# A decoder layer on one core: shared experts moved into the recurrence bodies, Gram products moved ahead, one tile pipeline over both parts, another order of the first loads

## The reference

```
q, k, v = silu(dwconv(hs @ W.T))                       # 4 heads of 64; beta = sigmoid(hs @ Wb.T)
# delta rule in chunks: A = tril(kb @ k.T, -1); Tinv = (I + A)^-1; u = Tinv @ v; w = Tinv @ kb
u_i = u_i - w_i @ S;  o_i = q_i @ S + attn @ u_i;  S = S + k_i.T @ u_i
wgt = softmax(gelu([hs, short.mean, long.mean, delta.mean] @ fg_w1.T + b1) @ fg_w2.T + b2)
x = x + rmsnorm(wgt0*short + wgt1*long + wgt2*delta + wgt3*v) @ Wo.T
x = x + cross_attention(layernorm(x), ctx)             # 16 heads of 16
# experts: sigmoid router, top 2 of 8, each y_e = (silu(x @ G_e.T) * (x @ U_e.T)) @ D_e.T, times the mean
# weight of expert e; two shared experts take every row
x = x + sum_e(sel_e * y_e * wmean_e) + shared(layernorm(x))
```

## Time and profile before

| what | value |
|---|---|
| median of the timed runs | 1503.44 us |
| profiled execution, whole / span | 1505.3 / 1503.2 us |
| PE matmul busy, span share | 1132.4 us, 75% |
| DVE busy | 867.0 us, 58% |
| POOL busy | 554.8 us, 37% |
| ACT busy | 454.0 us, 30% |
| mean granted clock of PE | 0.887 of 2.4 GHz |
| DMA | 124.56 MB, mean 83 GB/s |

### The profile page before, as it was taken

The page is one execution under the profiler, slowest core; times in us unless marked ns, Lnnn a source line. Parts: engine busy times, 40 slices in busy tenths (PEclk is TensorE's granted clock), DMA queues, the critical chain, the costliest instruction groups (busy, mean ns, idle before and its releaser), DMA issues. The chain is left out here.

```text
span 1503.2 us, 21723 instructions
## 1 busy us (share of the span) xinstructions
PE 1132.4 (75%) x7496; PEld 854.1 (57%) x7496; DVE 867.0 (58%) x2140; ACT 454.0 (30%) x818; POOL 554.8 (37%) x948
## 2 busy tenths in 40 slices
PE   1888878392993895797498399299389699788996
PEld 0455557371872773575476286287276567567553
DVE  1887844253755655566466476475567555543555
ACT  1766644222212322312312222221231244323110
POOL 2233434437018217415433542721822120303064
PEclk9998889696997897799699599699689899998999
DMA  6344342501002102000200210210200533446174
GB/s 160 91 142 136 118 123 89 173 1 56 15 2 102 43 1 99 33 10 31 87 29 29 70 43 15 88 43 1 70 29 29 211 118 97 159 136 211 50 232 142
DMA packets 85786, 124.56 MB, mean 83 GB/s; under 512 B 29040, under 2 KB 64112, under 8 KB 83504
## 3 DMA queue, kind: packets, MB, share of 16 engines
q1 hardware_dynamic: 78768, 104.30, 21.4%
q0 software_dynamic: 6912, 18.88, 3.9%
HBM read 66.91 MB, written 56.24 MB: 82 GB/s over the span
## 5 line engine op out<-in xcount | busy, mean ns | idle before, releaser
L900 ACT ACTIVATE arena<-bank 128x512 f32<-128x512 f32 (+2 forms) x318 | 166.3, 544 | 541.7 <-PE bank L541 132.2
L388 PE MATMUL bank<-const,arena 128*128 128x128 f32 x256 | 42.6, 321 | 212.4 <-DVE arena L1840 166.0
L388 PEld LDWEIGHTS bank<-const,arena 128*128 128x128 f32 x256 | 34.2, 164 | 219.1 <-DVE arena L1840 168.9
L1411 DVE SCALAR_TENSOR_TENSOR arena<-arena,param 128x512 f32<-128x512 f32 x144 | 106.1, 749 | 35.8 <-ACT arena L923 32.2
L405 PE MATMUL bank<-hsT,wt 128*128 128x512 f32 x192 | 100.5, 681 | 24.2 <-ACT hsT L900 24.2
L1283 POOL TENSOR_TENSOR arena<-arena 128x126 f32<-128x126 f32 (+22 forms) x248 | 101.0, 407 | 22.2 <-DVE arena L1482 3.3
L1270 POOL COPY arena<-arena 32x512 f32<-32x512 f32 x32 | 33.8, 1056 | 192.9 <-DVE arena L1472 191.4
L1335 POOL DMA_INDIRECT arena<-slots_y,arena x64 | 61.6, 962 | 114.2 <-DVE xt L1932 60.4
L1285 POOL TENSOR_TENSOR arena<-arena 128x126 f32<-128x126 f32 (+22 forms) x248 | 93.7, 378 | 19.4
L609 PEld LDWEIGHTS bank<-arena 128*128 128x128 f32 x768 | 88.6, 192 | 5.9 <-issue 5.7
L609 PE MATMUL bank<-arena 128*128 128x128 f32 x768 | 89.3, 275 | 0.0
(11 more groups left out here) (262 smaller groups left out, 2706.9 us busy)
## 6 DMA issues: line engine op xcount, KB each, us to landing
arena<-slots_x SPq DMA_DIRECT2D x78, 128.0 KB, 2.1
slots_y<-arena SPq DMA_DIRECT2D x78, 128.0 KB, 1.7
xt<-x_in SPq DMA_DIRECT2D x16, 512.0 KB, 5.5
kq_T<-kq SPq DMA_DIRECT2D x8, 1024.0 KB, 3.9
kq<-kq_T SPq DMA_DIRECT2D x8, 1024.0 KB, 7.3
vT<-v_T SPq DMA_DIRECT2D x8, 514.0 KB, 3.9
hs_T<-hsT SPq DMA_DIRECT2D x8, 512.0 KB, 4.2
v_T<-vT SPq DMA_DIRECT2D x8, 512.0 KB, 4.2
```

Of the source, the lines that this page charges most:

```text
L388: last = tr(o[:, t * P:(t + 1) * P], src[:, t, c * P:(c + 1) * P], ident)
L900: free(act.activation(out_, in_, func, **kw), name)
L1411: ins = V.scalar_tensor_tensor(cv[:, k % 4, :], pre[:, j, d:d + GT], param[:, at + d:at + d + 1], cv[:, k % 4, :], ALU.mult, ALU.add)
```

## The change

Four edits, one file.

*Shared experts.* `late_in` and `late_out` (PE), `late` and `late_added` (DVE), `late` (ACT) do the shared experts of group i-1 inside body i, behind the router, from the rows that are still in `xnT`; the sum is added to `xt` before it is stored (`rows_added`). The weights are loaded again in each body into a free half of `attnT` (`late_w`). The stores and loads of `xnT` in DRAM, `shared`, and `load_fx` go away.

*Gram products and recursion.* Steps t = 0 and 1 of the loop do two Gram products each. POOL copies the diagonal blocks tile by tile (16 copies in place of 4), clears them behind the `pow`s, and computes the router's norm factor within the recursion, behind step k = 15. The recursion of group 0 runs on DVE (`first_solve`).

*One tile pipeline.* Tiles 0 to 77 run without a break; DVE adds one 128-row piece of the final sum in 15 of the last steps (`PIECES`), the other 17 pieces follow.

*Start.* Rows of group 0 and the first 1536 columns of `wt` are loaded first; PE and ACT wait for less; POOL's first norm factor comes ahead of its 61 tap copies; DVE scales weights and masks behind the first convolution.

```diff
-    "gram_ready": 16, "diag_ready": 4, ...
+    "gram_ready": 16, "diag_ready": 16, ...
@@ PE
-            pe.wait_ge(w_loaded, 16 * 3)
-            pe.wait_ge(setup_dve, N_DVE_SETUP)
-            pe.wait_ge(setup_pool, N_POOL_SETUP)
             hidden_rows(0)
+            pe.wait_ge(first_loaded, 16)
...
+            def late_in(i, up_banks):
+                pe.wait_ge(sem("late_w_loaded"), 16 * min(i + 1, NG - 1))
+                for s_, at in (("lg", 0), ("lu", 1)):
+                    for e in range(2):
+                        n = f"{s_}{e}.{i}"
+                        w_ = expert(i, e)[at]
+                        k = up_banks[e] if at else None
+                        o = open_bank(pe, n, next(cross_bank) if k is None else k)
+                        for c in range(CK):
+                            last = mm(o[:, :], w_[:, c, :], xnT[:, c, :], start=c == 0, stop=c == CK - 1)
+                        full(last, n)
+            def late_out(i, banks_):
+                for e in range(2):
+                    drained(pe, f"lu{e}.{i}")
...
                 for t in range(T):
-                    if ahead:
-                        front_gram(i + 1, t)
+                    if ahead and t < 2:
+                        front_gram(i + 1, 2 * t)
...
                     if t < 2:
                         gate_hidden(0, 1 + t)
+                        if ahead:
+                            front_gram(i + 1, 2 * t + 1)
...
+                filters(2)
+                filters(3)
                 if x:
                     routing()
-                filters(2)
-                filters(3)
+                    late_in(i - 1, (7, None))
+                    late_out(i - 1, (2, 3))
                 pe.wait_ge(sem("on_ready"), i + 1)
@@ ACT, body
                 done(act.activation(gw[:, 1, :, :], gw[:, 0, :, :], ACT.Exp), "exp_ready")
+                if x:
+                    late()
+                    router()
...
-                if ahead:
-                    front_blocks(i + 1)
-                if x:
-                    router()
                 for c in range(CK):
                     n = f"oT{c}.{i}"
                     o = filled(act, n)
                     evac(h1T[:, c, :], o[:, :], n)
+                if ahead:
+                    front_blocks(i + 1)
@@ POOL
-                if x is not None:
-                    norm_scale(1, "x", 2 * x + 2)
+            def front_steps(i, x=None):
                 pool.wait_ge(sem("units_ready"), i + 1)
                 for k in range(QB - 1, 0, -1):
...
+                    if k == 15 and x is not None:
+                        norm_scale(1, "x", 2 * x + 2)
@@ DVE
                 dve.wait_ge(sem("gate_ready"), 2 * i + 2)
+                if x:
+                    routing()
                 for t0 in range(0, T, 2):
...
                 if x:
-                    routing()
+                    late()
...
                 done(ins, "on_ready")
                 if x:
+                    late_added()
                     ranks(i - 1)
...
             long_turned(0)
             front_units(0)
+            first_solve()
             long_turned(1)
...
+                if n in PIECES:
+                    combines(1)
```

More of the change, by code:

```diff
@@ L45 @@
 TILE0 = (0, NTILE[0], NTILE[0] + NTILE[1])
+PIECES = tuple(s for s in range(TILE0[1] + 5, TILE0[2] + 1) if s % 6)
 NWORD3 = (max(NTILE) + 2) // 3
@@ L872, in _ @@
             routing()
-            steps(4)
+            steps(2)
+            late_in(NG - 1, (None, None))
+            steps(2)
+            late_out(NG - 1, (None, None))
             positions(NG - 1)
-            steps(NTILE[0] + 3 - 31)
-            tile_experts(1)
-            for s_ in range(-2, NTILE[1] + 1):
-                tile_step(1, s_)
+            steps(8)
             n = "weights.0"
-            for i in range(NG):
-                shared(i)
-                if i == 0:
-                    o = open_bank(pe, n, next(cross_bank))
-                    pe.wait_ge(sem("route_sums"), 1)
-                    full(mm(o[:, 0:E], cst("ones"), gw[:, 0, :, :].rearrange("p t k -> p (t k)")[:, 0:E],
-                            start=True, stop=True), n)
+            o = open_bank(pe, n, next(cross_bank))
+            pe.wait_ge(sem("route_sums"), 1)
+            full(mm(o[:, 0:E], cst("ones"), gw[:, 0, :, :].rearrange("p t k -> p (t k)")[:, 0:E],
+                    start=True, stop=True), n)
+            steps(TILE0[2] + 1 - at_step[0])
         @block.scalar
@@ L1025, in router, with late @@
                          "scores_ready")
-                return rows, probs, routing, router
+                def late():
+                    for e in range(2):
+                        n = f"lg{e}.{i}"
+                        o = filled(act, n)
+                        evac(late_g[i][e], o[:, :], n, ACT.Silu)
+                return rows, probs, routing, router, late
             def body(i, x, ahead):
                 if x:
-                    rows, probs, routing, router = x
+                    rows, probs, routing, router, late = x
                 for t in range(T):
@@ L1132, in steps @@
                 for _ in range(k):
-                    tile_step(0, at_step[0])
+                    tile_step(at_step[0])
                     at_step[0] += 1
-            rows, probs, routing, router = cross(NG - 1)
+            rows, probs, routing, router, late = cross(NG - 1)
             steps(5)
@@ L1590, in routing, with late, late_added @@
                                          prm("lb").unsqueeze(1).broadcast_to([P, T, E]), ALU.add), n)
-                return masks, rows2, anykey, queries, context, scores, values, row_stats, rows3, routing
+                def late():
+                    for e in range(2):
+                        n = f"lu{e}.{i}"
+                        o = filled(dve, n)
+                        drained(dve, f"lg{e}.{i}")
+                        free(V.tensor_tensor(late_h[i][e], o[:, :], late_g[i][e], ALU.mult), n)
+                def late_added():
+                    for k in range(2):
+                        n = f"ld{k}.{i}"
+                        o = filled(dve, n)
+                        dst = rows[:, 2 * k:2 * k + 2, :]
+                        free(V.tensor_tensor(dst, dst, o[:, :].rearrange("p (t d) -> p t d", t=2), ALU.add), n)
+                    for k in range(2):
+                        drained(dve, f"ld{k}.{i}")
+                    done(V.memset(spare[:, :], 0.0), "rows_added")
+                return (masks, rows2, anykey, queries, context, scores, values, row_stats, rows3, routing, late,
+                        late_added)
             def ranks(i):
@@ L1693, in body @@
                 if x:
-                    masks, rows2, anykey, queries, context, scores, values, row_stats, rows3, routing = x
+                    (masks, rows2, anykey, queries, context, scores, values, row_stats, rows3, routing, late,
+                     late_added) = x
                     masks()
@@ L1867, in _ @@
                 body(i, cross(i - 1) if i else None, i + 1 < NG)
-            masks, rows2, anykey, queries, context, scores, values, row_stats, rows3, routing = cross(NG - 1)
+            (masks, rows2, anykey, queries, context, scores, values, row_stats, rows3, routing, late,
+             late_added) = cross(NG - 1)
             NT_ = NG * T
```

384 lines of the change are left out of this document (185 added, 199 removed).

## The result

The changed kernel takes 1465.5 us (median of four executions, 1463.6 to 1470.5) beside 1503.3 us for the kernel before on the same chip: ratio 0.9754, 95% interval 0.9727 to 0.9781. The forecast was 1468. The time came out close, but two of its terms were wrong by much and in opposite directions, so the profile has to be read term by term. The profiled execution took 1463.9 us.

A forecast was written before the change was run, and what follows sets the result against it. Four limits in turn: a late start, waiting chains in the bodies, PE in the tiles, PE then DVE at the end. Terms -16+0-3+39+0+11-66 = -35 us against 1503.2 gave 1468, range 1437 to 1491.

The forecast's parts named there:

- start, until the first Gram product: Start: early rows let PE begin at about 12.8 us, 19.6 earlier; after DVE's scaling and SP's store, -16 us.
- first recursion, until the first N: Group 0's recursion on DVE: 17.7 us against 28.6 on POOL, but transposes stand behind it, so 0 us gained.
- body 0: Body 0: no cross part, only the earlier recursion; -3 us (bounds 0 and -4).
- bodies 1 to 6: Bodies 1 to 6: recursion 4.4 us earlier, yet each body longer by 6.5 us; +39 (bounds +11 and +54).
- tiles, until the first gather: Tiles: group 7's shared experts (10.6 us, 1.6 hidden), weight sums and the filled pipeline delay the first gather, +11 us.
- end: First gather to end: POOL's gathers limit at 1.25 us each; 86.6 us instead of 152.5, -66.
- The factor: Bodies 1 to 6: router's norm factor behind k = 15 moves turned rows, gate and mix back by 13.5 us.
- Earlier recursion: Body 3: with memsets and factor out of its way, the recursion starts 4.4 us earlier, despite 0.9 for paired Gram products.
- The mix: Body 3: DVE's mix starts at 724.1 and its factors are done at 734.0 us in the trace, after router and filters.
- `late_out`: Body tail on PE: shared experts' second matmuls, behind `late` and ahead of the mixed rows, charged 5.9 us.
- The signs: Marks expected in the profile after: first N at 270 to 272, row norm waiting 12 to 14 us, bodies of 124 to 129.
- light-bodies rival: Bodies: shared matmuls keep PE at full clock and a body costs only 1.8 us or less; total 1440, chance 0.2.

The follow-up runs named there:

- Kernel 8: Changed kernel with the rows of groups 0 and 1 issued behind weights, masks and start rows again: 1509.6 us, beside 1498.5 for the changed kernel rerun.
- kernel 4: Changed kernel with the first group's recursion on GpSimd again instead of DVE: 1494.1 us, beside 1498.5 for the changed kernel rerun.
- kernel 1: Changed kernel with the router's norm factor behind step k = 28 of the recursion instead of k = 15: 1470.0 us, beside 1498.5 for the changed kernel rerun.
- kernel 3: Changed kernel with one Gram product in each of the four steps instead of pairs: 1484.1 us, beside 1498.5 for the changed kernel rerun.
- kernel 2: Changed kernel with the norm factor behind k = 28, `late` ahead of DVE's compaction and ACT's placing ahead of its copies: 1463.2 us, ratio to before 0.9548.
- 10: Changed kernel with early factor, `late` and placing first, single Gram products, first recursion on GpSimd and tile numbers read word by word: 1443.0 us, ratio to before 0.9419.
- kernel 11: As kernel 10, but the mixed rows' two pow inside GpSimd's recursion, compaction behind `late_added`, ACT's copies first again: 1436.5 us, ratio to before 0.9378.
- Kernel 6: Changed kernel without the shared experts of groups 0 to 6 in the bodies (not the whole layer): 1482.6 us, beside 1498.5 for the changed kernel rerun.
- kernel 7: Changed kernel with all 32 pieces of the final sums behind the last tile: 1517.7 us, beside 1498.5 for the changed kernel rerun.
- kernel 9: The changed kernel unedited, run again on a later chip: 1498.5 us, ratio to before 0.9789.

## Why the forecast came out, and where it was wrong

The sum was -35, the profiled execution shows -41.1. By the forecast's steps:

| step | forecast | measured |
|---|---|---|
| start, until the first Gram product | -16 | -15.0 |
| first recursion, until the first N | 0 | +2.7 |
| body 0 | -3 | -1.4 |
| bodies 1 to 6 | +39 | +14.7 |
| body 7, until the first tile | 0 | +1.5 |
| tiles, until the first gather | +11 | +19.5 |
| end | -66 | -63.2 |

- **Start: right.** PE at 12.57 (12.8 said). Kernel 8 shows that 12.4 of the 19.9 us are the early rows. That every engine waits for the last mask and the last weights, as my opening has it, is the smaller part: without the early rows the start gains only about 7 us.
- **First recursion: the mechanism right, the size off.** I worked out 17.7 us for DVE; it took 19.8, and the compaction came 3.4 us later than the 266.0 I had: 2.1 us by the length, the rest because the recursion began 15.2 us earlier than before (237.69 against 252.97) and not 17. That the transposes behind it eat the gain is what kernel 4 shows.
- **The factor: right.** I said 18 us behind the recursion's start and a wait of 12 to 14; it was 17.5 and 14.8, and the turned rows moved by 14.3 us behind N (13.5 said). Half clock there: as said, but it costs less. I charged 2.8 us for transposes and logits; they took 1.97 and 2.71 instead of 1.09 and 1.95, 1.6 together, for the full clock is back within the logits. The mix began at 102.5 behind N, I had 103.6. That the gate had slack of just that size was not right: kernel 1 takes the wait away and a body gets 5 us shorter.
- **Earlier recursion: right, 3.8 us instead of 4.4.** The forecast took the Gram pairs for +0.9 us; kernel 3 has them at 1.5 to 2.4. I then credited them with the 3.8 in kernel 3's expectation, though the page said otherwise.
- **The mix: mis-sized.** I carried over 9.9 us from its first product to the factors. It took 8.0 in the changed kernel. Neither before nor after does DVE stand idle within it; some of its own operations got shorter. Groups of DVE from 340 to 1200 us (busy, mean ns of one), two of the kernel before, two of the changed one, one of kernel 1:
```profile
L1819 DVE SCALAR_TENSOR_TENSOR arena<-arena,gw 128x256 f32<-128x256 f32 x32 | 18.7, 623 | 0.0
L1815 DVE SCALAR_TENSOR_TENSOR arena<-bank,gw,arena 128x256 f32<-128x256 f32 x32 | 13.8, 472 | 0.0
...
L1894 DVE SCALAR_TENSOR_TENSOR arena<-arena,gw 128x256 f32<-128x256 f32 x30 | 13.5, 491 | 0.0
L1890 DVE SCALAR_TENSOR_TENSOR arena<-bank,gw,arena 128x256 f32<-128x256 f32 x29 | 12.6, 474 | 0.0
...
L1894 DVE SCALAR_TENSOR_TENSOR arena<-arena,gw 128x256 f32<-128x256 f32 x30 | 18.0, 638 | 0.0
```
  The products with both inputs in the arena (SBUF) were slow in the kernel before, where the mix ran beside GpSimd's longest recursion steps (120 to 136 elements). With the factor late the mix lies beside the last, short steps and behind the recursion, and they are fast; those that read a PSUM bank don't change. Kernel 1 moves the mix back beside the long steps, and it takes 9.9 us again. Kernels 1, 2, 10 and 11, with the factor early, all have 9.7 to 9.9 in body 3; the changed kernel, 3 and 6 have 8.0. The filters, which the change moved ahead of the mix in all of them, make no such difference. Mix and factors were done at 110.4 behind N, I had 113.5.
- **`late_out`: mis-sized, and its return left out of the bound.** I charged 5.9 us; it took 5.1 in body 3 and 5.1 to 5.4 in all six bodies. (In the later runs some bodies have up to 6.8, on each of the three chips.) The full clock it hands on to mixed rows and projection I did count. Together, with compaction and `late` 0.3 us shorter than I had, the mixed rows start at 117.3 and not at 121.5: 1.1 us by the clock ahead of the mix and what follows it, 1.9 by the mix, 0.3, and 0.9 by late_out. These 4.2 us in body 3 are the error of a body, 4.0 on the mean. Kernel 6 confirms the account from the other side: taking all shared work out shortens a body by 1.4 us only.
- **The tiles: a step missing.** Nothing of the 10.6 us of group 7's matmuls was hidden (I let 1.6), and SyncE's reading of the tile numbers had been harmless when part 0 was drained before part 1; a pipeline that runs through made it a hole of 5.7 us. I had put 1.5 on that boundary. The first two tiles run at half clock (two transposes 0.66 us instead of 0.41), 1.3 us that I hadn't counted, and the 1 us that I took off for the stores doesn't show.
- **The end: right.** Gathers are the limit, without a gap, 1.27 us each instead of 1.25, and kernel 7 shows that they need the pieces where they are.
- **The signs.** First N at 274.8 (270 to 272 said) and a body of 122.9 us (124 to 129 said) both missed, the one late and the other short, and the row norm's wait, 14.8 us, lies just above its 12 to 14. The others came as said. Why body 0 gained 1.4 us and not 3, and body 7 lost 1.5, was not followed up.

So the total came close because bodies 1 to 6 were over-charged by 24 us and all other steps together under-charged by 18. That the two cancel is luck. The light-bodies rival (1.8 us a body) was nearest to what the bodies do, while its total of 1440 is not, for the same reason.

The Trainium skill (TensorE: Matmul & The Clock Gate, What's actually happening) puts the cost of the ramp under 1% of a typical kernel's span. The rows don't bear that out as a rule for a kernel with chains like this one, where the half clock comes back in each body: in kernel 2 the projection alone takes 6.35 us instead of 3.69 in body 3, in kernel 11 N takes 2.3 us more, and both come back in body 4 (6.0 us for the projection in kernel 2); six times 2.3 to 3.6 us is 1 to 1.5% of the span. The Trainium skill (GPSIMD Engine Reference, 4.1 Engine selection) has GpSimd about twice as slow for two-input elementwise work; here the first group's 62 operations take 19.8 us on VectorE and 28.6 on GpSimd (kernel 4, 239.77 to 268.34), a ratio of 1.4.

## What to carry to other kernels

Where a chain on one engine is made to carry a small step of another chain, put it where its input is just ready, not halfway: a factor of 1.3 us placed 13 us too late (92.6 us behind N, in kernel 1 79.4) moved an idle gap and cost 28 us in all. Before charging work that fills an idle gap at its full length, ask what clock the work behind it had without it. Before carrying over a length, ask what ran beside it on the other engines, and whether it still will. And when a drain between two phases is taken out, look for what the queues did in its shadow: register reads, waits for tables.

## What the runs showed of the hardware

- **Two places of the tiles, and 2% of the whole.** On the three later chips every kernel is slow at the same two places: from tile 28 to 36 it takes 28.2 to 29.1 us (17.4 in the first comparison), from tile 55 to 60 23.0 to 24.9 us (9.0). PE, ACT and DVE have waits there that nothing in the profile explains, while GpSimd's gathers go on every 1.25 us at the second. PE in kernel 9:
```profile
1402.65 0.48 PE L850 MATMUL bank<-const,arena 128*128 128x128 f32 x1 [3.23 <-issue]
1406.39 1.22 PE L855 MATMUL bank<-arena 128*128 x2 [3.27 <-issue]
1409.76 0.69 PE L835 MATMUL bank<-const,arena 128*128 128x128 f32 x2 [2.15 <-issue]
```
  These two places make 27 of the 33 us between the first comparison and kernel 9. What they are was not tried, and whether it is the chip at all stays open; the kernel before is 28 us slower there, with no trace of it to say where.
- **VectorE is slower beside GpSimd's recursion, the more the longer its steps.** Two products of the mix with both inputs in SBUF take 1.1 to 1.3 us together in body 3 before, beside steps of 120 to 136 elements, and 0.87 in the changed kernel, beside steps of 16 and 30 or none; the two that read a PSUM bank take 0.86 to 0.88 in both. The row norm, 128x256 with one tensor operand, takes 1.38 us for four beside steps of 30 and 31 elements (before), 1.68 beside 78 and 81 (kernel 1), 2.08 beside 126 and 130 (changed). The Trainium skill (GPSIMD Engine Reference, 1. Specifications) says that GpSimd shares its access to SBUF with VectorE, and names VectorE's instructions with two SBUF inputs among those that contend; the rows of the mix agree, though no run measured the pair by itself.
